# A mixture-of-experts layer on token rows sorted by expert, in a two-layer Trainium2 kernel

## What is computed

```python
logits = flat_x @ W_router + b_router            # (2048, 8)
top_vals, top_idx = jax.lax.top_k(logits, 2)
sparse_logits = neg_inf.at[jnp.arange(T)[:, None], top_idx].set(top_vals)
router_weights = jax.nn.softmax(sparse_logits, axis=-1)
for e in range(8):
    expert_mask = jnp.any(top_idx == e, axis=-1)
    h = jax.nn.relu(flat_x @ W1[e] + b1[e])      # 512 hidden channels
    y = h @ W2[e] + b2[e]
    w = router_weights[:, e] * expert_mask.astype(x.dtype)
    final_output = final_output + y * w[:, None]
```

## Time and profile before

| | us |
|---|---|
| median of 3 runs (lowest, highest) | 2101.96 (2100.68, 2103.45) |
| the profiled execution | 2103.51 |
| its span, first to last instruction | 2101.8 |
| projection, norm and router of the last sublayer, 1784.7 to 1843 | 58.3 |
| its experts, 1843 to 2087 | 244.0 |
| last norm, 2087 to the end | 14.8 |

### The profile page before, as it was taken

How to read it: one execution, slowest core, us unless ns; L and a number is a source line. 1 busy time by engine, 2 the same in 40 slices (tenths; PEclk the granted TensorE clock), 3 DMA queues, 4 the chain that set the end, 5 groups by cost and what they waited for, 6 DMA issues and landing times. The chain is left out here.

```text
span 2101.8 us, 42721 instructions
## 1 busy us (share of the span) xinstructions
PE 1853.7 (88%) x16342; PEld 1538.4 (73%) x16342; DVE 1407.1 (67%) x3137; ACT 986.4 (47%) x2509; POOL 525.9 (25%) x889
## 2 busy tenths in 40 slices
PE   3699999899999999999946979999999999789996
PEld 2578777787877788787734647888888887657675
DVE  4688877778877777788736756666666666333334
ACT  2355555555555555555523246656656655111111
POOL 6254533455453345545310000000000000000000
PEclk9799999999999999999966989999999999889998
DMA  5223233322322342232301000000000000200000
GB/s 187 59 52 77 62 69 79 79 58 54 75 63 68 79 78 62 50 75 64 69 22 70 0 0 1 1 2 1 1 2 1 2 2 2 81 1 1 0 0 20
DMA packets 100374, 87.77 MB, mean 42 GB/s; under 512 B 12804, under 2 KB 90584, under 8 KB 99160
## 3 DMA queue, kind: packets, MB, share of 16 engines
q1 hardware_dynamic: 100184, 85.19, 16.1%
HBM read 81.71 MB, written 3.45 MB: 41 GB/s over the span
## 5 line engine op out<-in xcount | busy, mean ns | idle before, releaser
L344 PE MATMUL ps<-xT,taps 128*128 128x128 f32 x2176 | 295.2, 279 | 0.1
L344 PEld LDWEIGHTS ps<-xT,taps 128*128 128x128 f32 x2176 | 275.9, 197 | 8.0 <-issue 7.6
L576 POOL TENSOR_TENSOR kfull<-kt,pair_rows 128x512 f32<-128x512 f32 x128 | 143.7, 1123 | 514.2 <-ACT kt L364 504.3
L829 ACT COPY wt<-ps 32x128 f32<-32x128 f32 x512 | 131.2, 256 | 259.9 <-PE ps L725 253.4
L1544 DVE TENSOR_REDUCE b_nmax<-ps 128x1 f32<-128x128 f32 (+7 forms) x256 | 180.6, 752 | 72.9 <-PE ps L1394 72.9
L872 DVE TENSOR_TENSOR prod<-ps,mt 128x128 f32<-128x128 f32 x512 | 147.3, 288 | 74.5 <-PE ps L736 59.2
L1521 POOL COPY b_spread<-b_inv 128x256 f32<-128x256 f32 x64 | 25.6, 401 | 666.6 <-DVE b_inv L1547 666.6
L725 PE MATMUL ps<-ident,w 128*128 128x128 f32 x512 | 162.3, 317 | 34.2 <-ACT wt L829 19.8
L1151 PEld LDWEIGHTS ps<-f_w,f_hT 128*128 128x128 f32 x1408 | 166.3, 192 | 31.9 <-issue 23.6
L1137 PE MATMUL ps<-xTn,f_w 128*128 x352 | 167.7, 612 | 24.8 <-PEq L1046 18.5
L1151 PE MATMUL ps<-f_w,f_hT 128*128 128x128 f32 x1408 | 167.8, 276 | 0.9 <-DVE f_hT L1214 0.8
(11 more groups left out here) (207 smaller groups left out, 3808.6 us busy)
## 6 DMA issues: line engine op xcount, KB each, us to landing
decay<-ends_dram SPq DMA_DIRECT2D x256, 128.0 KB, 5.8
gn<-near_dram SPq DMA_DIRECT2D x34, 384.0 KB, 7.0
rr<-rates_dram SPq DMA_DIRECT2D x34, 256.0 KB, 4.6
sq<-rstd_dram SPq DMA_DIRECT2D x17, 512.0 KB, 3.7
wtap<-in_taps SPq DMA_DIRECT2D x4, 1024.0 KB, 11.7
f_w<-in_f_w SPq DMA_DIRECT2D x2, 2048.0 KB
near_dram<-near_rows SPq DMA_DIRECT2D x17, 96.0 KB, 1.6
f_w<-in_f_w SPq DMA_DIRECT2D x2, 768.0 KB, 5.3
```

The lines of the kernel that those rows point to most:

```text
L344: mm = pe.matmul(part, lhsT=taps[:, tap, t * P:(t + 1) * P], rhs=xT[:, :, columns(at_next) - LOOK + tap:columns(at_next) - LOOK + tap + TS ...
L576: nc.gpsimd.tensor_tensor(kfull[:, n % 4, :, :], kt[:, n % 2, :].unsqueeze(1).to_broadcast([P, G, P]), cst["pair_rows"][:, :].unsqueeze(2) ...
```

## The change

The three functions `project_out`, `layer_norm` and `route` are no longer called for the last sublayer, nor is `experts`. One new function, `sparse_experts`, does all of it in one block, with the four groups of four tiles (`s`) pushed through projection, norm and router one behind the other.

Two arrays in DRAM, `x_dram` and `y_dram`, have 2048 slots for each expert and 1024 more. Both are filled with zeros by two DMAs of SP during the softmax attention. For each token and each of its two experts, `place_rows` counts the token's place among those of that expert (a product with a triangular matrix, `before`, and running sums in `seen`), which gives its slot. POOL stores the rows there: 32 indirect DMAs, each of 128 rows of 512 bytes (`slot_i` has the row numbers). `make_table` works out which 128 slots each of 39 blocks covers and its expert. 39 is 4096 / 128 plus 7 for blocks that are not full. The blocks then run in order: SP reads the block's address from the table and loads 128 rows, TensorE turns them (`turn_block`), multiplies by four tiles of w1 (`up`) and by four of w2 (`down`), VectorE copies the block's weights out of the expert's place to a fixed one (`stage`, since the expert is known only when running), and POOL stores the result to the same slots of `y_dram`. After all 39, POOL issues 32 indirect loads that bring each token's two result rows back, and `mix` adds them with their weights. The bias b2 is added for all tokens ahead of the blocks.

The core of the new function:

```diff
+        with nc.Block() as block:
+            @block.sync
+            def _(sp):
...
+                sp.wait_ge(S["table_done"], 1)
+                sp.wait_ge(S["x_out"], 16 * NT * TOP)
+                for k in range(BLOCKS):
+                    if k >= 4:
+                        sp.wait_ge(S["x_turned"], k - 3)
+                        sp.wait_ge(S["staged"], k - 3)
+                    at = sp.value_load(table_i[0:1, 0, k:k + 1], min_val=0, max_val=(NE * SLOTS) + (NE - 2) * P)
+                    sp.dma_start(xb[:, k % 4, :], x_dram[bass.ds(at, P), :]).then_inc(xb_in[k % 4], 16)
...
+            @block.gpsimd
+            def _(pool):
...
+                for s in range(PARTS):
+                    pool.wait_ge(S["slotted"], s + 1)
+                    pool.wait_ge(S["row_kept"], TOP * (s + 1))
+                    for n in range(GT * s, GT * s + GT):
+                        for w in range(TOP):
+                            nc.gpsimd.indirect_dma_start(
+                                out=x_dram[:, :], out_offset=bass.IndirectOffsetOnAxis(ap=slot_i[:, n, w:w + 1], axis=0),
+                                in_=row_of(n, w), in_offset=None).then_inc(S["x_out"], 16)
+                pool.wait_ge(S["table_done"], 1)
+                for k in range(BLOCKS):
+                    pool.wait_ge(S["y_kept"], k + 1)
+                    at = pool.value_load(table_i[0:1, 0, k:k + 1], min_val=0, max_val=(NE * SLOTS) + (NE - 2) * P)
+                    nc.gpsimd.dma_start(y_dram[bass.ds(at, P), :], yb[:, k % 4, :]).then_inc(y_out[k % 4], 16)
+                for k in range(4):
+                    pool.wait_ge(y_out[k], 16 * len(range(k, BLOCKS, 4)))
+                for n in range(NT):
+                    for w in range(TOP):
+                        nc.gpsimd.indirect_dma_start(
+                            out=yl[:, n, w, :], out_offset=None, in_=y_dram[:, :],
+                            in_offset=bass.IndirectOffsetOnAxis(ap=slot_i[:, n, w:w + 1], axis=0)).then_inc(yl_in[n // GT], 16)
...
+            @block.tensor
...
+                turn_block(0)
+                for k in range(BLOCKS + 1):
+                    if k + 1 < BLOCKS:
+                        turn_block(k + 1)
+                    if k < BLOCKS:
+                        up(k)
+                    if k >= 1:
+                        down(k - 1)
...
+            @block.vector
...
+                def stage(k):
+                    if k >= 2:
+                        dve.wait_ge(S["down_done"], k - 2)
+                        dve.wait_ge(S["up_done"], k - 1)
+                    if k >= 3:
+                        dve.wait_ge(S["rect_a"], k - 2)
+                    e = dve.value_load(table_i[0:1, 1, k:k + 1], min_val=0, max_val=NE - 1)
+                    nc.vector.tensor_copy(w1s[:, k % 2, :], w1[:, bass.ds(e * F1, F1)])
+                    nc.vector.tensor_copy(w2s[:, k % 3, :, :], w2[:, bass.ds(e * J, J), :])
+                    nc.vector.tensor_copy(b1s[:, k % 3, :], b1[:, bass.ds(e * J, J)]).then_inc(S["staged"], 1)
...
+                def keep_y(k):
+                    dve.wait_ge(S["down_done"], k + 1)
+                    if k >= 4:
+                        dve.wait_ge(y_out[k % 4], 16 * (k // 4))
+                    nc.vector.tensor_copy(yb[:, k % 4, :], ps[:, k % 2, 0:C]).then_inc(S["y_kept"], 1)
...
+                for k in range(BLOCKS):
+                    if k + 1 < BLOCKS:
+                        stage(k + 1)
+                    rectify(k)
+                    if k >= 1:
+                        keep_y(k - 1)
+                keep_y(BLOCKS - 1)
```

```diff
+                sp.wait_ge(fill_made, 1)
+                for rows in blank[1:]:
+                    rows = rows.rearrange("(k p) e -> p k e", p=P)
+                    sp.dma_start(rows, blank[0][:, :].unsqueeze(1).to_broadcast([P, rows.shape[1], C])).then_inc(filled, 16)
+                sp.wait_ge(filled, 32)
```

More of the change, by code:

```diff
@@ L7 @@
 BF16 = mybir.dt.bfloat16
+I32, U32 = mybir.dt.int32, mybir.dt.uint32
 ALU = mybir.AluOpType
@@ L951, in _ @@
                         dve_piece(dve, ch, only_post, f, 1, q, NS - 2 + f)
+        stage_end(nc, every)
 def layer_norm(nc, ctx, cst, ps, res, xT, name, loads=(), arrived=(), out=None):
@@ L1257, with softmax_attention @@
 TT = T // P
-def softmax_attention(nc, ctx, cst, ps, weights, xT, yT):
+def softmax_attention(nc, ctx, cst, ps, weights, xT, yT, blank):
     HD = AH * AD
@@ L1515, in _ @@
                 keep_recips(W - 1)
+            @block.sync
[5 more added lines that the diff above has]
+                sp.wait_ge(filled, 32)
             @block.gpsimd
             def _(pool):
+                nc.gpsimd.memset(blank[0][:, :], 0.0).then_inc(fill_made, 1)
                 for w in range(W):
@@ L1561, in softmax_attention @@
         stage_end(nc, every)
[L1564 to L1588, removed]
+F1 = 512
@@ L1591 @@
 F0_WIDTHS = [128] * 4 + [256] * 4
-F1_WIDTHS = [512] * NE
+F1_WIDTHS = [F1] * NE
 def program(nc, d, out):
@@ L1626, in program @@
         yT = sb("b_yT", [P, NP, B * T])
-        softmax_attention(nc, ctx, cst, ps, (wdown, wq, wkv), xT, yT)
+        zero = sb("zero", [P, C])
+        x_dram = nc.dram_tensor("slots_dram", (NE * SLOTS + NE * P, C), F32).ap()
+        y_dram = nc.dram_tensor("out_rows_dram", (NE * SLOTS + NE * P, C), F32).ap()
+        softmax_attention(nc, ctx, cst, ps, (wdown, wq, wkv), xT, yT, (zero, x_dram, y_dram))
         ff = sum(F1_WIDTHS)
@@ L1630, in program @@
         b1, b2, br = sb("f1_b1", [P, ff // P]), sb("f1_b2", [NE, C]), sb("f1_br", [P, NE])
[L1631 to L1638 removed]
+        route_pairs = [(wr[:, :], d["f1_wr"]), (br[:, :], d["f1_br"].partition_broadcast(P))]
+        f1_pairs = [(b1[:, :], d["f1_b1"]), (b2[:, :], d["f1_b2"]), (w1[:, :].rearrange("c (e f) -> c e f", e=NE), d["f1_w1"]),
+                    (w2[:, :, :], d["f1_w2"])]
+        sparse_experts(nc, ctx, cst, ps, wout, yT, res, xT, (w1, w2, wr, b1, b2, br), (route_pairs, f1_pairs),
+                       (x_dram, y_dram), out)
 def lay_out(i):
```

359 lines of the change are left out of this document (350 added, 9 removed).

## The result

The changed kernel takes 2020.1 us (median of 4 runs, 2017.1 to 2023.2) against 2102.7 us on the same chip (4 runs): a ratio of 0.9607, 95% interval 0.9589 to 0.9625. The forecast was 2058 us with a range of 1990 to 2125; the sign and the range hold, and the gain is 82.6 us where 44 were forecast, nearly double. The profiled execution took 2023.2 us for a span of 2021.3.

A forecast was written before the change was run, and what follows sets the result against it. The experts were taken as TensorE's own time; of the 155 us it saves, 35 go to blocks that VectorE sets, 50 to the gather, 27 to stores and first load, the rest to ends: 2058 us, range 1990 to 2125.

The forecast's parts named there:

- What bounded the kernel, and what goes: Experts: TensorE's own time; 39 blocks of nine products at 0.233 us take 82 us against 237, so 155 us go.
- Routing and projection: Ahead of the stores: some 3 us between projection pieces, projection ends at 1818.4, VectorE's chain gives last slots at 1845.
- the semaphore clear: After the first stage: new clear with its barrier costs what the one ahead of the projection did, 1.6 us.
- rival 3: Blocks stay at the slow clock: 2 x 2.1 = 4.2 us each, 47 us more, 2105; chance 0.09.
- Stores to slots: 32 indirect DMAs on POOL at 1.5 us each; the last 24 queue for 36 us, landed at 1868.
- Blocks: Block loop: VectorE is the bound at 3.0 us a block, 39 take 117 us, 4 us to fill and drain.
- no round trip within one period: Block loop: behind `rectify(k)` wait only block k's products down, nine products later on TensorE.
- Last store and gather: After the blocks: last store 3.5 us, then 32 indirect loads on POOL, 48 us and 2 us landing, to 2045.5.
- Tail: Last part's mixes and norm after the gather: 7 us, to 2052.5, then 2.4 us to the end of the span.
- Rival 1: Blocks: POOL's y stores held through VectorE's copies, 3.8 us replace 3.0, 31 us more, 2089; chance 0.13.
- Rival 2: Stores and gather: indirect DMA dearer; at 2.3 us no gain left, at 2.8 us 73 us more, 2131; chance 0.17.
- Rival 4: Blocks at 2.3 us with register loads hidden, indirect DMAs at 0.9 us: 27 + 34 us less, 1997; chance 0.17.

The follow-up runs named there:

- The run with the other TensorE order: Changed kernel with the third projection ahead of part 0's turn and logits and the fourth ahead of its positions: 2010.8 us.
- the orders after it: Further reorderings between projection and stores: on the changed kernel 2005.2 us; with indirect y stores in the block loop as well 1982.4, then 1983.0 and 1978.7 us.
- the extra copy: Changed kernel with a third 128x512 copy on VectorE in each block, to a tile nobody reads: 2027.1 us, one run.
- the early load: Kernel of 1978.7 us (reordered front, y stored indirectly in the loop), with the next expert number loaded behind the three copies: 1974.4 us, the fastest version.
- The scatter: Changed kernel with y stored to token rows by indirect stores inside the block loop and four plain loads replacing the 32 indirect loads: 1996.3 us.

## Why the forecast gain was low, step by step

**What bounded the kernel, and what goes.** Right. The experts were TensorE's time, and 39 blocks cost TensorE 74 us at full clock where 82 were reckoned: 1.90 us each, not 2.10. The 0.233 us for a product came from a mean over 512; here four products take 0.89 us, 0.222 each, and the transpose 0.11, not a product's price.

**Routing and projection: missed.** The forecast had the projection end at 1818.4 and the last slots at 1845; they came at 1840.1 and 1867.0. Of this 2.7 us lie ahead of the projection, which began at 1789.2 instead of 1786.6; the forecast had 1.6 of them in another term, the semaphore clear. The failing step is "some 3 us between its pieces". It counted what TensorE executes there, not what it waits for: two round trips over VectorE and ScalarE, and a loop in which `project(3)` waits for `choose(0)`, which waits for `project(2)`. The run with the other TensorE order gave 9 us of this back, the orders after it more. At these gaps the clock fell as well. With 3.24 and 5.72 us of idle TensorE ahead it was granted 0.74 from 1810 to 1820 and 0.67 from 1820 to 1841, and the same 64 instructions took 9.8 and 10.1 us that take 7.39 at 1.00 in the run without the wait. The stretch of the earlier trace rows showed that fall, and it was put only in the blocks (rival 3), not here.

**Stores to slots.** The mechanism held: a chain on POOL that does not wait for landings. A call takes 1.27 us against 1.5 forecast, within the bounds 0.9 and 2.9; both bounds were guesses round a missing row, so the hit is in part luck. The chain of the last 24 stores started 22 us late and was 6 us shorter; the first block's rows were turned at 1886.2, against 1872.6 reckoned with the 1.6 us of the semaphore clear, so that front and stores together cost 13.6 us more than reckoned.

**Blocks: the mis-sized term that made the gain double.** The forecast was 3.0 us with VectorE as the bound, between 2.2 and 3.7. It is 1.92 us, below even the lower end, which was TensorE's time as forecast. VectorE is a bound as forecast, without a wait for others, but only by some 0.03 us over TensorE's 1.90. From the first turn at 1886.2 to the last y at about 1964 are 78 us where 121 were reckoned, 43 us less, more than the 35 by which the whole sum was too high. VectorE's operations were right, 1.64 us against 1.67, but that sums durations: operations in a row start before the one ahead has ended by its row (0.34 us apart for 0.43), and together they fill 1.37 us of a block. The load with its semaphores was taken at 1.1 us, by a row of a DMA that has little to do with it; it is 0.55. The 0.2 us of waiting didn't exist. So VectorE needed 1.37 + 0.55 = 1.92 us where 3.0 had been put: 42 us over 39 blocks, of which the load's price is 21, the overlap 12, the waiting 8 and rounding 1. TensorE, expected busy near 70%, is shown busy 99%.

The "no round trip within one period" was right. The Trainium skill, DMA: Bandwidth & Descriptors, section "Latency and other measured facts", gives a `tensor_load` a floor of about 600 ns; the hole of 0.55 us here is near it and a little below. The 0.27 us in some blocks with the extra copy, and no hole ahead of the copies with the early load, say that other work can cover it.

**Last store and gather.** The last y landed and the gather began at 1968.6; from there to the last landing it took 42.4 us where 50 were reckoned, the difference being again a call, 1.29 us in the mean against 1.5. The scatter showed the rest of the step right: the 32 calls stood on the path, since with the stores hidden in blocks the kernel got 23.8 us shorter, the plain loads and VectorE's mixes, no longer beside the calls, taking the rest.

**Tail.** 7.6 us against 7.0, and 2.75 to the end against 2.5. The fills landed 28.5 and 53.6 us after their issue, inside the softmax stage, with nothing waiting.

The sum: +13.6 (front and stores), -43 (blocks), +0.5 (last store), -7.6 (gather), +0.9 (tail) make -35.6, and 2056.6 less 2021.3 is 35.3.

**Rivals.** Rival 1, POOL locked by VectorE's copies: no. POOL's store took 0.542 us in the mean and never set a block. The row of 6.28 us didn't show such a lock either, though the prediction read it so: in the same rows the operation at 10.14 took its 0.53 us beside that memset, begun at 7.92, and the long one ended at 17.3, 2.5 us after it. What held it stays open. The Trainium skill's rule (SBUF — State Buffer, "SBUF: two separate sides") that such a DMA is starved of its descriptors doesn't show in the times of these stores; with a third copy to each block they took 0.557 us, and they landed after 1.8 us in both kernels. What the runs show of the two engines is rather the reverse, VectorE's copy at 0.556 us beside POOL's indirect store. Rival 2, an indirect DMA of 2.3 us or more: no, 1.265. Rival 3, blocks at the slow clock: only for about 5 us, granted 0.5 at the first block and 1.00 three blocks later; its kind of cost fell on the projection instead. Rival 4, cheap all round, had the right direction in both terms, 2.3 us a block and 0.9 us a call giving 1997. The blocks were cheaper still, and the front and the call dearer.

## What to carry to other kernels

Count an engine's load by the spacing of starts in a row of like operations, not by the sum of durations. Don't take TensorE's busy share for a proof that it is the bound: it read 40.00 of 40 us with blocks of 1.90, 1.92 and 1.99 us, and the count of instructions and the holes in the weight loads told them apart. Bound a register load by rows near in kind, not by a DMA that lands. Where stages are interleaved, follow each wait through all queues that it stands in: one product group behind one wait kept three engines and the clock down, and freeing one part moved the wait to the next until every queue was put in the order of need. A chain of fixed-price calls on a slow queue (1.27 us each here) belongs beside work that is there anyway: 39 stores inside the loop in place of 32 loads behind it gave 24 us back.

## What the runs showed of the hardware

An indirect DMA on POOL costs 1.27 us (stores) to 1.29 us (loads) from start to start for 128 rows of 512 bytes, 0.98 of it busy, and 0.93 busy for 64 rows: a price per call as far as these two sizes show. It lands 2.2 us (store) to 2.5 us (load) after its issue, and POOL doesn't wait for that.

A VectorE copy of 128x512 float32 between SBUF tiles took 0.56 us instead of 0.42 at the end of POOL's indirect store, 0.46 at the start of one (the fastest version), and 0.42 in the kernel with POOL's plain store.

A register load on VectorE leaves a hole of 0.55 us when it stands ahead of the instructions that need it, and 0.19 us in the mean when it stands behind 0.9 us of copies: VectorE goes on with what was issued to it earlier.

TensorE was granted the lower of its two levels (1.2 GHz, 0.50 from 1888 to 1890) after the 17 us of idle time ahead of the first block, and was back at 2.4 GHz (1.00 from 1892 on) some 5 us after that block had begun.
